# Softmax attention of 16 heads: natural units ahead of the exponentials' units, value products in up to two pieces, transposes at a chunk's end

## The chip, the core and the metric

The kernel runs on one core of one Trainium2 chip, as one launch. The time is device time in microseconds (us) of that core, and less is better. The engines named below are TensorE (PE), VectorE (DVE), ScalarE (ACT), GpSimd (POOL) and SyncE (SP), which issues DMAs.

## The reference

Four layers follow one another on x of (2, 1024, 256); the change touches the first, a differential softmax attention with 16 heads of 2 x 8 query and key columns and 16 value columns:

```python
q1, k1, q2, k2, v = jnp.split(layernorm(x) @ Wqkv, [C, 2 * C, 3 * C, 4 * C], axis=-1)
A1 = causal_sdpa(q1, k1, v)          # per head: softmax(mask(q k^T / sqrt(8))) @ v
A2 = causal_sdpa(q2, k2, v)
diff = A1 - lam * A2                 # then an RMS norm per head, and diff @ Wproj
```

After it come a routed feed-forward layer, a memory attention and a ternary feed-forward layer.

## The kernel before, in words

`attention_heads` works head by head; each engine runs its own `period(h)` for h = 0 to 15. A head has four sets: two batches b and two attentions j. The operands of j = 0 lie in partitions 0 to 63 and those of j = 1 in partitions 64 to 127 (`SIDE` = 64), so their matmuls use different row halves of TensorE.

**Natural units** (tile `nat`, three PSUM buffers) give the row maxima of the head that comes next. `unit_scores` makes one: q k^T with queries in partitions (line 644), and for a block on the diagonal two small matmuls that add the mask (line 648). DVE reduces each one (line 516, `mpart`). There are 40 to a head, alternately j = 1 (even numbers) and j = 0 (odd). When all 40 are reduced, DVE takes the head's maxima (`negm`, line 520), PE turns them (line 656), DVE splits them in three bf16 parts (lines 531 to 539), and SP moves the parts into rows of the queries, so that the exponentials' scores come out with the maximum subtracted. After that DVE goes on with the next natural units. PE starts unit u only when DVE has reduced unit u - 3.

**Units for the exponentials** (tile `sc`, two PSUM buffers) are made by `scores(h, n, c)` (line 682): keys in partitions, 9 chunks n = 0 to 8 of 512 columns, four sets c = 0 to 3 each, with j = 0, 1, 0, 1. ACT makes the exponential of each (line 611, into `PT`), and PE starts one only when the exponential of the unit two before it is done.

**Value products** (`values(h, n)`, line 702) multiply `PT` of a whole chunk with the head's values, fp32, into `OT`, all four sets side by side in column groups of 32. They come two chunks late (`VLAG` = 2): in chunk n PE does the value products of chunk n - 2, and in chunks 0 and 1 those of chunks 7 and 8 of the head before. POOL masks the diagonal chunks 0, 2, 4, 7 and 8 first (line 481). Most chunks are one segment of 512 columns; chunk 2 is 384 + 128, chunk 4 is 256 + 256, chunk 8 is 384 + 128.

When the last value products of a head are done, ACT copies `OT` out (`OTS`, line 593, after the exponentials of chunk 1), PE turns it in two halves of four **transposes** (`turn_outputs`, line 718, tile `misc`), and ACT copies each half (`ONS`, line 600) after the exponentials of chunks 2 and 3. The first value products of the new head write `OT` again, so they too wait for `OTS`.

The order on PE is written out by hand in `period`: in each of the 36 steps (n, c) a unit for the exponentials, then one natural unit (two in four of the steps: n, c = 2, 0; 4, 1; 6, 2; 8, 3), and after c = 1 the transposes (in chunks 2 and 3) and the value products. In the generator `maxima`, the turn of `negm` comes ahead of the third natural unit after a head's last, in chunk 6.

Of the kernel before, what the change touches and what calls it, by code (L numbers as in the profile page):

```python
# [351 lines left out]
def attention_heads(nc, K):  # L352
# [5 lines left out]
    NU, NCH = len(units), len(PROB_CHUNKS)  # L358
    FIRST, GAP = (2 * NU) // 5, 2
    VLAG = 2  # L360
    with ExitStack() as ctx:
# [26 lines left out]
        class Head:  # L388
# [8 lines left out]
            def next(self, d):  # L397
                return Head(self.i, self.k + d)
# [8 lines left out]
        def heads(eng, period):  # L407
            for n in range(H0):
                period(Head(0, n))

        @block.sync
        def _(sp):
            def maxima(h):

                hold(sp, s_msp, h.count(1, 1), K.s_held)
                for j in range(2):
                    for part in range(3):
                        row = SIDE * j + STK + part
                        sp.dma_start(QS[row:row + 1, h.buf, :].rearrange("a (r q) -> a r q", q=P),
                                     msplit[16 * j:16 * j + 16, part, :]).then_inc(s_mld, 16)  # L420

            def period(h):
                if h.next(2).exists():
                    if not isinstance(h.n, int) or h.n > 0:

                        hold(sp, s_sc, h.count(4 * NCH), K.s_held)
                    later = h.next(2)
                    load_head(sp, K, later.n, later.buf, slice(0, B * T), s_load[later.buf])
                if h.next(1).exists():
                    maxima(h.next(1))  # L430

            load_head(sp, K, 0, 0, slice(T, B * T), s_load[0])
            load_head(sp, K, 1, 1, slice(0, B * T), s_load[1])
            maxima(Head(0, 0))
            heads(sp, period)
# [190 lines left out]
        @block.tensor  # L626
        def _(pe):
            def unit_scores(h, u):

                head_0 = isinstance(h.n, int) and h.n == 0  # L630
                if u == 0 and head_0:
                    pe.wait_ge(K.s_first, 16 * HEAD_LOADS)
                if u == (NU // 2 if head_0 else 0):
                    pe.wait_ge(s_load[h.buf], 16 * HEAD_LOADS * (h.times + 1))

                if not isinstance(h.n, int) or NU * h.n + u > 2:
                    pe.wait_ge(s_max, h.count(NU, u - 2))
                b, j, segs = units[u]
                side, rows = slice(SIDE * j, SIDE * j + SIDE), slice(SIDE * j, SIDE * j + STK)
                for n, (i, k0, w) in enumerate(segs):  # L640
                    out = nat[:, (NU * h.k + u) % 3, n * w:(n + 1) * w]
                    q = b * T + i * P
                    diag = i * P - k0
                    ins = pe.matmul(out, QS[rows, h.buf, q:q + P], KS[rows, h.buf, b * T + k0:b * T + k0 + w],  # L644
                                    start=True, stop=diag >= w)
                    if diag < w:
                        for half, (unit, mask) in enumerate(((K.ident_bf, K.mask), (K.ident_swap, K.mask_swap))):
                            ins = pe.matmul(out[:, diag:diag + P], unit[side, :], mask[side, :], start=False, stop=half == 1)  # L648
                ins.then_inc(s_nat, 1)

            def turn_max(h):
                pe.wait_ge(s_negm, h.count(1, 1))

                if not isinstance(h.n, int) or h.n >= 2:
                    pe.wait_ge(s_ons, h.count(2, -2))
                pe.transpose(misc[0:32, 0:P], negm[:].rearrange("p j b i -> p (j b i)"), K.ident[:]).then_inc(s_mT, 1)

            def maxima(h):

                first, second = h.next(1), h.next(2)  # L660
                if not first.exists():
                    return
                for u in range(FIRST, NU):
                    unit_scores(first, u)
                    yield
                for u in range(FIRST):
                    if u == GAP or not second.exists():
                        turn_max(first)
                        if not second.exists():
                            return  # L670
                    unit_scores(second, u)
                    yield

            def scores(h, n, c):
                u = 4 * n + c
                j, b = SET_ORDER[c] // 2, SET_ORDER[c] % 2
                rows = slice(SIDE * j, SIDE * j + STK + 3)
                if not isinstance(h.n, int) or 4 * NCH * h.n + u > 1:
                    pe.wait_ge(s_exp, h.count(4 * NCH, u - 1))
                col = 0  # L680
                for kt, q0, w in PROB_CHUNKS[n]:
                    ins = pe.matmul(sc[:, u % 2, col:col + w], KS[rows, h.buf, b * T + kt * P:b * T + (kt + 1) * P],  # L682
                                    QS[rows, h.buf, b * T + q0:b * T + q0 + w], start=True, stop=True)
                    col += w
                ins.then_inc(s_sc, 1)

            def values(h, n):

                if n in DIAG_CHUNKS:
                    pe.wait_ge(s_msk, h.count(len(DIAG_CHUNKS), DIAG_CHUNKS.index(n) + 1))  # L690
                else:
                    pe.wait_ge(s_exp, h.count(4 * NCH, 4 * n + 4))
                if n == 0:
                    pe.wait_ge(s_vh, h.count(1, 1))

                    if not isinstance(h.n, int) or h.n > 0:
                        pe.wait_ge(s_ots, h.count(1))
                col = 0
                for kt, q0, w in PROB_CHUNKS[n]:
                    for c in range(4):  # L700
                        b = c % 2
                        ins = pe.matmul(OT[32 * c:32 * c + 32, q0:q0 + w], VH[:, h.buf, b * TB + kt, :],  # L702
                                        PT[:, n % 3, c, col:col + w], start=(kt == 0), stop=(kt, q0) in ((2, 256), (7, 896)),
                                        skip_group_check=True)
                    col += w
                ins.then_inc(s_pv, 1)

            def turn_outputs(h, r):
                if r == 0:
                    pe.wait_ge(s_ots, h.count(1, 1))  # L710

                    if h.next(1).exists():
                        pe.wait_ge(s_msp, h.count(1, 2))
                else:
                    pe.wait_ge(s_ons, h.count(2, 1))
                for k in range(4):
                    t = 4 * r + k
                    ins = pe.transpose(misc[:, k * P:(k + 1) * P], OTS[:, t * P:(t + 1) * P], K.ident[:])
                ins.then_inc(s_on, 1)

            def period(h):

                last, between = h.next(-1), maxima(h)

                pe.wait_ge(s_mld, h.count(96, 96))
                for n in range(NCH):
                    for c in range(4):
                        scores(h, n, c)
                        k = 4 * n + c
                        for _ in range(NU * (k + 1) // (4 * NCH) - NU * k // (4 * NCH)):  # L730
                            next(between, None)
                        if c == 1:
                            if last.exists() and VLAG <= n < VLAG + 2:
                                turn_outputs(last, n - VLAG)
                            if n >= VLAG:
                                values(h, n - VLAG)
                            elif last.exists():
                                values(last, NCH + n - VLAG)
                for _ in between:
                    pass  # L740

            for u in range(FIRST):
                unit_scores(Head(0, 0), u)
            for _ in maxima(Head(0, -1)):
                pass
            heads(pe, period)
            last = Head(0, H0 - 1)
            for n in range(VLAG):
                values(last, NCH + n - VLAG)
            for r in range(2):  # L750
                turn_outputs(last, r)
# [1704 lines left out]
```

## Time and profile before

| what | us |
|---|---|
| median of 3 runs | 1730.11 (1729.01 to 1734.66) |
| the profiled execution, its own time | 1742.41 |
| its span, first to last instruction | 1740.6 |
| stretch of the 16 heads, from the first to the last matmul of the loop | about 87 to 620 |
| one head in the middle, from one copy of `OTS` to the next | 30.98 to 31.00 |

Mean granted TensorE clock over the span: 0.926 of full speed. The profiled execution is 12.3 us above the median; differences that are worked out in its rows are subtracted from the median. The first columns of a timeline row are the start (us from the span's start) and the duration; merged rows have a count. Matmuls overlap, so the time that one takes from its neighbours is the distance from start to start, not its duration.

### The profile page before, as it was taken

The page shows a single profiled execution, that of the slowest core. Times are in us where ns is not written, and L with a number is a line of the kernel's source. Part 1 is how long each engine was busy: PE and PEld are TensorE (multiplying, and loading weights), DVE is VectorE, ACT ScalarE, POOL GpSimd, SP SyncE. Part 2 cuts the span into 40 slices and gives each one's busy share as a digit, 9 for nine tenths or more (in the row PEclk, how much of TensorE's full clock was granted, in tenths as well). Part 3 has the DMA queues.
Part 4 walks back from the last instruction along what each step waited for, and adds up shares of the span by engine and source line. Part 5 has one row for each costly group of instructions (what it writes and reads, how often), then busy time and mean ns, then how long its engine had stood idle before and what let it go on. Part 6 is the DMA issues. An engine that isn't in the chain of part 4 may idle for free. (4 is left out here: it accounts for less than half of the span.)

```text
span 1740.6 us, 27816 instructions
## 1 busy us (share of the span) xinstructions
PE 1491.9 (86%) x9044; PEld 1018.5 (59%) x9044; DVE 1261.2 (72%) x3421; ACT 1109.9 (64%) x2384; POOL 1086.0 (62%) x1283
## 2 busy tenths in 40 slices
PE   7898888888888855788856899999999999887998
PEld 4433333333333134575645788888788888776565
DVE  5778888888787025743365999999999999973433
ACT  3147767666676523403124899999999999994332
POOL 5105665655655554032243999999999999974353
PEclk9769999999999566999988999999999999999899
DMA  5301010010010041452100000000000100000000
GB/s 200 104 20 38 21 32 26 21 38 20 25 34 2 1 154 49 149 181 97 49 0 1 2 1 1 1 1 1 1 1 1 49 1 1 1 1 1 1 25 25
DMA packets 40137, 59.98 MB, mean 34 GB/s; under 512 B 9452, under 2 KB 33912, under 8 KB 39096
## 3 DMA queue, kind: packets, MB, share of 16 engines
q1 hardware_dynamic: 39992, 58.19, 10.4%
q8 instruction: 73, 1.20, 0.3%
q14 instruction: 72, 0.59, 0.1%
HBM read 40.93 MB, written 16.78 MB: 33 GB/s over the span
## 5 line engine op out<-in xcount | busy, mean ns | idle before, releaser
L611 ACT ACTIVATE a_PT<-a_sc 128x512 f32<-128x512 f32 x576 | 319.0, 599 | 209.7 <-PE a_sc L682 203.5
L516 DVE TENSOR_REDUCE a_mpart<-a_nat 128x1 f32<-128x512 f32 (+3 forms) x640 | 363.8, 628 | 87.5 <-PE a_nat L648 54.4
L2022 DVE BATCH_NORM_STATS2 c_stat<-c_R 128x6 f32<-128x512 f32 x576 | 381.1, 679 | 2.1 <-ACT c_R L1941 1.8
L1986 POOL TENSOR_SCALAR c_R<-big,c_negtau 128x256 f32<-128x256 f32 x264 | 301.4, 1168 | 34.6 <-DVE c_negtau L2055 29.0
L1986 POOL TENSOR_SCALAR c_R<-c_Z,c_negtau 128x256 f32<-128x256 f32 x255 | 291.5, 1169 | 14.9 <-DVE c_negtau L2088 14.9
L644 PE MATMUL a_nat<-mem 48*128 48x512 bf16 (+3 forms) x768 | 223.6, 356 | 25.2 <-DVE a_mpart L516 11.9
L682 PE MATMUL a_sc<-mem 51*128 51x512 bf16 (+3 forms) x768 | 207.0, 355 | 41.3 <-ACT a_PT L611 38.7
L481 POOL TENSOR_SCALAR_AFFINE_SELECT a_PT<-a_PT 128x512 f32<-128x512 f32 x128 | 79.4, 638 | 244.3 <-ACT a_PT L611 244.2
L1858 PE MATMUL c_z<-mem,c_R 128*128 128x256 f32 x1024 | 231.5, 379 | 0.0
L1941 ACT ACTIVATE c_R<-c_Z,c_negtau 128x256 f32<-128x256 f32 x513 | 216.0, 516 | 0.4 <-DVE c_negtau L2088 0.4
L1941 ACT ACTIVATE c_R<-big,c_negtau 128x256 f32<-128x256 f32 x504 | 212.6, 515 | 2.9 <-DVE c_negtau L2055 1.7
L1858 PEld LDWEIGHTS c_z<-mem,c_R 128*128 128x128 f32 x1024 | 192.9, 190 | 25.4
L702 PE MATMUL a_OT<-a_PT,a_VH 128*32 128x512 f32 (+3 forms) x1536 | 170.8, 543 | 0.6 <-POOL a_PT L481 0.6
L682 PEld LDWEIGHTS a_sc<-mem 51*128 51x128 bf16 x768 | 52.4, 95 | 197.6 <-ACT a_PT L611 158.1
L1870 PE MATMUL c_T<-ident,c_R 128*128 128x128 f32 x768 | 107.3, 283 | 36.0 <-ACT c_R L1936 35.4
L1858 PE MATMUL c_z<-mem,c_hT 128*128 128x256 f32 x512 | 119.9, 389 | 8.8 <-ACT c_hT L1965 8.8
L1882 PE MATMUL c_y<-mem,c_R 128*128 128x256 f32 x512 | 120.7, 386 | 0.0
L1870 PEld LDWEIGHTS c_T<-ident,c_R 128*128 128x128 f32 x768 | 86.5, 143 | 56.6 <-ACT c_R L1936 46.7
L1936 ACT ACTIVATE c_R<-c_T 128x512 f32<-128x512 f32 x192 | 104.2, 596 | 22.7 <-PE c_T L1870 22.7
L1858 PEld LDWEIGHTS c_z<-mem,c_hT 128*128 128x128 f32 x512 | 99.0, 195 | 24.5 <-ACT c_hT L1965 9.3
L644 PEld LDWEIGHTS a_nat<-mem 48*128 48x128 bf16 x768 | 68.1, 97 | 71.0 <-DVE a_mpart L516 50.4
L648 PE MATMUL a_nat<-mask,ident_bf 64*128 64x128 bf16 x512 | 106.9, 231 | 0.0
(316 smaller groups left out, 2638.6 us busy)
## 6 DMA issues: line engine op xcount, KB each, us to landing
mem<-qk_parts SPq DMA_DIRECT2D x360, 32.0 KB
qk_parts<-a_parts SPq DMA_DIRECT2D x16, 384.0 KB, 2.6
made<-f_made SPq DMA_DIRECT2D x24, 256.0 KB, 2.8
mem<-made SPq DMA_DIRECT2D x3, 2048.0 KB, 8.4
X<-in_L_attn_x_dram SPq DMA_DIRECT2D x4, 512.0 KB, 6.9
mem<-in_L_ffn_wq_dram SPq DMA_DIRECT2D x1, 2048.0 KB, 14.4
ternary<-f_W_T SPq DMA_DIRECT2D x1, 2048.0 KB, 6.3
mem<-in_L_ffn_wo_dram SPq DMA_DIRECT2D x1, 2048.0 KB, 12.6
```

The source lines that it names most:

```text
L516: dve.tensor_reduce(dst, src, AX.X, ALU.max).then_inc(s_max, 1)
L611: act.activation(PT[:, n % 3, SET_ORDER[c], :], sc[:, u % 2, :], ACT.Exp, scale=SCALE0).then_inc(s_exp, 1)
L644: ins = pe.matmul(out, QS[rows, h.buf, q:q + P], KS[rows, h.buf, b * T + k0:b * T + k0 + w], start=True, stop=diag >= w)
L648: ins = pe.matmul(out[:, diag:diag + P], unit[side, :], mask[side, :], start=False, stop=half == 1)
L682: ins = pe.matmul(sc[:, u % 2, col:col + w], KS[rows, h.buf, b * T + kt * P:b * T + (kt + 1) * P], QS[rows, h.buf, b * T + q0:b * T + q0 + ...
L702: ins = pe.matmul(OT[32 * c:32 * c + 32, q0:q0 + w], VH[:, h.buf, b * TB + kt, :], PT[:, n % 3, c, col:col + w], start=(kt == 0), stop=(kt ...
L1858: ins = pe.matmul(z_ps[:, n % SCORE_BANKS, e * NMEM:(e + 1) * NMEM], L, G[:, m, h, :], start=(m == 0), stop=(m == 1))
L1870: ins = pe.transpose(T_ps[:, n % TURN_BANKS, (2 * e + m) * P:(2 * e + m + 1) * P], whole(i, h)[:, m * P:(m + 1) * P], K.ident[:])
L1882: ins = pe.matmul(y_ps[:, k % 2, 0:D], weights(i, h, m), K.VO[:, m, h, :], start=(n == 0), stop=(n == 15))
L1941: act.activation(split(i, h) if r < NR else whole(i, h), scores_of(i)[:, h, :], ACT.Relu, bias=threshold(i, r, h)).then_inc(s_ra[r], 1)
L1986: pool.tensor_scalar(split(i, h) if r < NR else whole(i, h), scores_of(i)[:, h, :], threshold(i, r, h), 0.0, ALU.add, ALU.max).then_inc(s_ ...
L2022: dve.bn_stats(stat[:, r, b, :], R[:, slot(i), b, :]).then_inc(s_stat, 1)
```

## The change

In each step the natural unit now stands ahead of the unit for the exponentials. The value products are a generator that stops between segments: the first piece is issued after c = 1, the second, where there is one, after c = 2. Only chunks 2, 4 and 8 have a second piece; with the delay of two chunks these fall in chunks 4, 6 and 1. The transposes move from ahead of the value products to the end of the chunk.

```diff
             def values(h, n):
+                for _ in value_pieces(h, n):
+                    pass
+
+            def value_pieces(h, n):
...
                     col += w
+                    if col < 512:
+                        yield
                 ins.then_inc(s_pv, 1)
...
                 for n in range(NCH):
+                    pieces = value_pieces(h, n - VLAG) if n >= VLAG else value_pieces(last, NCH + n - VLAG) if last.exists() else iter(())
                     for c in range(4):
-                        scores(h, n, c)
                         k = 4 * n + c
                         for _ in range(NU * (k + 1) // (4 * NCH) - NU * k // (4 * NCH)):
                             next(between, None)
-                        if c == 1:
-                            if last.exists() and VLAG <= n < VLAG + 2:
-                                turn_outputs(last, n - VLAG)
-                            if n >= VLAG:
-                                values(h, n - VLAG)
-                            elif last.exists():
-                                values(last, NCH + n - VLAG)
+                        scores(h, n, c)
+                        if c in (1, 2):
+                            next(pieces, None)
+                    if last.exists() and VLAG <= n < VLAG + 2:
+                        turn_outputs(last, n - VLAG)
```

No instruction is added or removed. Two places of PE's order show it.

PE in chunk 2, from c = 1 to the next chunk's c = 0. Before (`nat` is a natural unit, `sc` one for the exponentials in two segments, `misc` the transposes, `OT` the value products):

```order
L682 MATMUL a1_sc<-mem3 128x384 [waits a1_exp]
L682 MATMUL a1_sc<-mem3 128x128
L644 MATMUL a1_nat<-mem3 128x512 [waits a1_max]
L718 MATMUL a1_misc<-ident,a1_OTS 128x128 [waits a1_msp,a1_ots]
L718 MATMUL a1_misc<-ident,a1_OTS 128x128 x3
L702 MATMUL a1_OT<-a1_PT,a1_VH 32x512 [waits a1_ots,a1_vh,a1_msk]
L702 MATMUL a1_OT<-a1_PT,a1_VH 32x512 x3
L682 MATMUL a1_sc<-mem3 128x384 [waits a1_exp]
L682 MATMUL a1_sc<-mem3 128x128
L644 MATMUL a1_nat<-mem3 128x512 [waits a1_max]
```

The same place in the changed kernel, up to the transposes:

```order
L682 MATMUL a1_sc<-mem3 128x384 [waits a1_exp]
L682 MATMUL a1_sc<-mem3 128x128
L706 MATMUL a1_OT<-a1_PT,a1_VH 32x512 [waits a1_ots,a1_vh,a1_msk]
L706 MATMUL a1_OT<-a1_PT,a1_VH 32x512 x3
L644 MATMUL a1_nat<-mem3 128x512 [waits a1_max]
L682 MATMUL a1_sc<-mem3 128x384 [waits a1_exp]
L682 MATMUL a1_sc<-mem3 128x128
L644 MATMUL a1_nat<-mem3 128x512 [waits a1_max]
L682 MATMUL a1_sc<-mem3 128x384 [waits a1_exp]
L682 MATMUL a1_sc<-mem3 128x128
L724 MATMUL a1_misc<-ident,a1_OTS 128x128 [waits a1_msp,a1_ots]
L724 MATMUL a1_misc<-ident,a1_OTS 128x128 x3
```

The value products now take the first wait for `OTS`, and the four transposes stand two natural units and two units for the exponentials later, ahead of the next chunk.

PE in chunk 6, from the value products on. Before:

```order
L702 MATMUL a1_OT<-a1_PT,a1_VH 32x256 x7
L682 MATMUL a1_sc<-mem3 128x512 [waits a1_exp]
L644 MATMUL a1_nat<-mem3 128x512 [waits a1_max] x2
L682 MATMUL a1_sc<-mem3 128x512 [waits a1_exp]
L644 MATMUL a1_nat<-mem3 128x512 [waits a1_max]
```

And in the changed kernel:

```order
L706 MATMUL a1_OT<-a1_PT,a1_VH 32x256 [waits a1_msk]
L706 MATMUL a1_OT<-a1_PT,a1_VH 32x256 x3
L644 MATMUL a1_nat<-mem3 128x512 [waits a1_max] x2
L682 MATMUL a1_sc<-mem3 128x512 [waits a1_exp]
L706 MATMUL a1_OT<-a1_PT,a1_VH 32x256 x4
L644 MATMUL a1_nat<-mem3 128x512 [waits a1_max]
L682 MATMUL a1_sc<-mem3 128x512 [waits a1_exp]
```

Both natural units of the double step now stand ahead of the unit for the exponentials, and the second half of the value products behind it.

## Rows read from the trace of the kernel before

**Rows 1.** Busy time in a stretch: PE, PEld, DVE, ACT, POOL, granted clock, DMA.

```profile
300.00:400.00 100.00, 88.22 (x857) 38.50 (x855) 80.60 (x161) 68.38 (x127) 58.74 (x95) 0.97 0.10 26
```

**Rows 2.** Waits of PE from 120 to 600 us: total, times, longest.

```profile
PE a_sc L682 <- ACT a_PT L611: 36.4, 91, 0.8
PE a_misc L718 <- ACT a_OTS L593: 4.3, 15, 0.3
```

**Rows 3.** Timeline of PE in one head: chunk 1 to chunk 4, and into chunk 5.

```profile
320.37 1.07 PE L702 MATMUL a_OT<-a_PT,a_VH 128*32 128x384 f32 x16
...
323.85 0.66 PE L718 MATMUL a_misc<-ident,a_OTS 128*128 128x128 f32 x4 [0.29 <-ACT a_OTS L593]
324.43 1.06 PE L702 MATMUL a_OT<-a_PT,a_VH 128*32 128x512 f32 x8
325.43 0.40 PE L682 MATMUL a_sc<-mem 51*128 51x384 bf16 x4
...
326.51 0.39 PE L682 MATMUL a_sc<-mem 51*128 51x512 bf16 x1 [0.46 <-ACT a_PT L611]
...
327.00 0.39 PE L682 MATMUL a_sc<-mem 51*128 51x512 bf16 x1
...
328.23 1.06 PE L702 MATMUL a_OT<-a_PT,a_VH 128*32 128x512 f32 x8
...
331.57 1.07 PE L702 MATMUL a_OT<-a_PT,a_VH 128*32 128x384 f32 x16
...
334.59 1.07 PE L702 MATMUL a_OT<-a_PT,a_VH 128*32 128x512 f32 x8
```

**Rows 4.** Timeline of ACT in the same head.

```profile
321.79 1.08 ACT L611 ACTIVATE a_PT<-a_sc 128x512 f32<-128x512 f32 x2 [0.78 <-PE a_sc L682]
322.76 1.03 ACT L593 ACTIVATE a_OTS<-a_OT 128x1024 f32<-128x1024 f32 x1
...
325.86 1.08 ACT L611 ACTIVATE a_PT<-a_sc 128x512 f32<-128x512 f32 x2 [1.08 <-PE a_sc L682]
```

**Rows 5.** Timeline of PE behind the value products of chunk 4.

```profile
332.58 0.28 PE L682 MATMUL a_sc<-mem 51*128 51x256 bf16 x1
332.58 0.28 PE L644 MATMUL a_nat<-mem 48*128 48x256 bf16 x1
332.70 0.27 PE L682 MATMUL a_sc<-mem 51*128 51x256 bf16 x1
```

**Rows 6.** Timeline of PE one head earlier: chunk 6 to chunk 0.

```profile
306.74 1.07 PE L702 MATMUL a_OT<-a_PT,a_VH 128*32 128x256 f32 x16
...
308.77 0.39 PE L644 MATMUL a_nat<-mem 48*128 48x512 bf16 x1 [0.64 <-ACT a_PT L611]
...
310.88 1.06 PE L702 MATMUL a_OT<-a_PT,a_VH 128*32 128x512 f32 x8
...
314.04 1.07 PE L702 MATMUL a_OT<-a_PT,a_VH 128*32 128x512 f32 x8
...
317.37 1.07 PE L702 MATMUL a_OT<-a_PT,a_VH 128*32 128x512 f32 x8
```

**Rows 7.** Timeline of DVE in that stretch.

```profile
308.04 4.26 DVE L516 TENSOR_REDUCE a_mpart<-a_nat 128x1 f32<-128x512 f32 x7
```

**Rows 8.** Timeline of ACT in that stretch.

```profile
308.17 0.60 ACT L611 ACTIVATE a_PT<-a_sc 128x512 f32<-128x512 f32 x1 [0.72 <-PE a_sc L682]
...
309.73 0.41 ACT L614 ACTIVATE a_Wabs<-Wb 128x256 f32<-128x256 bf16 x1
```

**Rows 9.** Timeline of ACT, the copies of `OTS` in the two heads that follow.

```profile
356.61 1.03 ACT L593 ACTIVATE a_OTS<-a_OT 128x1024 f32<-128x1024 f32 x1
387.60 1.03 ACT L593 ACTIVATE a_OTS<-a_OT 128x1024 f32<-128x1024 f32 x1
```

**Rows 10.** PE in a stretch: busy time, granted clock, DMA.

```profile
345.00:349.00 4.00, 4.00 (x22) 0.50 0.02 4
```

**Rows 11.** Timeline of PE in that stretch, the value products of chunk 6.

```profile
346.55 1.93 PE L702 MATMUL a_OT<-a_PT,a_VH 128*32 128x512 f32 x8
348.41 0.80 PE L682 MATMUL a_sc<-mem 51*128 51x384 bf16 x3
```

## The prediction

> **What bounds the kernel now.** I read first the busy times of a stretch of the heads: TensorE 88 of 100 us, DVE 81, ACT 68, POOL 59, at a granted clock of 0.97 [rows 1]. No engine is full, so each waits for others in turn. The list of TensorE's waits then says for whom: 36.4 us in 91 waits for exponentials, and 4.3 us in 15 waits for the copy of the outputs [rows 2]. The timelines of one head show where these fall.
>
> I count a head by its value products; V(n) are those of chunk n. One head: V(8) at 320.37, V(0) at 324.43, V(1) at 328.23, V(2) at 331.57, V(3) at 334.59 [rows 3]; a head earlier V(4) at 306.74, V(5) at 310.88, V(6) at 314.04, V(7) at 317.37 [rows 6]. The distances are 4.06, 3.80, 3.34, 3.02, then 4.14, 3.16 and 3.33.
>
> The distance of a plain chunk is a loop through ACT, not TensorE's work. From V(0): the value products hold the array from 324.43 to 325.43, 1.00 us. The next unit for the exponentials starts at 325.43; its exponential starts at 325.86, 0.43 later [rows 4]. Two exponentials take 1.08, so the second starts 0.48 after the first and lasts 0.60. It ends at 326.94, and the unit for c = 1 of the next chunk starts at 327.00, 0.06 later [rows 3]. With one natural unit more the next V could follow, at 1.00 + 0.43 + 1.08 + 0.06 = 2.57 plus 0.3 to 0.6. Before c = 0 TensorE stood idle, a wait of 0.46 by the row at 326.51. So the transposes, 0.58 us ahead of V(0) and as much ahead of V(1) (323.85 to 324.43 [rows 3]), stand on the loop where nothing covers them, while 0.46 us of idle time lie half a chunk later.
>
> Chunks 5 to 7 are different: DVE does seven natural units without a gap from 308.04, 0.61 each [rows 7], after it has split the maxima. TensorE waits for it.
>
> **The change part by part.** No instruction comes or goes, DMAs are untouched, and POOL and SP keep their places. I follow the new order with the durations above. Two more are needed. Value products take 1.00 at full clock and 346.55 to 348.41 = 1.86 at the granted clock of 0.50 [rows 10, 11]. So 0.86 scales with the columns and 0.14 does not: a piece of 384 columns takes 0.64 + 0.14 = 0.78, one of 128 takes 0.36, one of 256 takes 0.57. A natural unit or one for the exponentials holds its row half for 0.22 (estimate from the four that fill 325.43 to 326.3), one with masks 0.33. I allow 0.1 for entering value products or transposes.
>
> *A, V(8) to V(0), 4.06 before.* The transposes leave: -0.58. V(0) now has the wait for `OTS` itself. V(8) comes in pieces of 384 and 128. The first lets the unit c = 2 start 0.22 earlier, but the second piece and its entry, 0.46, stand ahead of c = 3. Its exponential starts 0.78 + 0.22 + 0.46 + 0.43 = 1.89 after V(8), against 321.79 + 0.48 - 320.37 = 1.90 now. `OTS` is no earlier [rows 3, 4]. A = -0.58.
>
> *B, V(0) to V(1), 3.80 before.* The natural unit that now comes first is odd (j = 0), on the same row half as the unit c = 2, so that one starts at 1.22. Exponentials at 1.65 and 2.13, end 2.73; unit c = 1 at 2.79, V(1) at 2.79 + 0.32 = 3.11. The transposes (0.56 and 0.2 for entry and exit) are issued at 1.55, finish near 2.3 and delay c = 0 (ready at 2.31) hardly. B = -0.69.
>
> *C, V(1) to V(2), 3.34 before.* The same loop with masks, start of c = 2 at 1.33, gives 3.2, and now the second transposes stand in it: TensorE is nearly full. C = -0.14.
>
> *D, V(2) to V(3), 3.02 before.* The second piece delays c = 3, and V(3) comes at 3.28. But DVE takes the outputs' small operations and four short units there, and in my follow-through its next long unit starts at 4.8 after V(2), as before. D = +0.04, bounds -0.1 and +0.27.
>
> *E, chunk 6.* The trace has natural unit 5, second of the double step, waiting until 308.77 for DVE (the row's releaser names ACT; it starts 0.05 after DVE's unit 2 ends, 308.04 + 0.68) [rows 6, 7]. Behind it on TensorE stands c = 3 now. After the change c = 2 does too: its exponential, at 308.17 before [rows 8], comes at 308.77 + 0.22 + 0.43 = 309.4. Then comes the second piece of V(4), to 309.88, the unit c = 3 at 310.1, its exponential 310.5 to 311.1, with ACT's operation for the ternary weights (0.41 [rows 8]) behind it. So c = 1 of chunk 7 starts at 311.17 and V(5) at 311.5, against 310.88. DVE takes up part of it, since its backlog ends near 312.3 in either order: V(6) comes at 314.6 against 314.04. E = +0.55, bounds 0 and +0.8.
>
> *F, V(6) to V(8).* In chunks 8 to 1 c = 1 has no natural unit between it and the value products, which saves the 0.11 of the masks once or twice; a natural unit ahead of c = 2 can cost as much. F = -0.1, bounds -0.3 and +0.3.
>
> Sum for a head: -0.58 - 0.69 - 0.14 + 0.04 + 0.55 - 0.1 = -0.92. It holds 14 times (heads 1 to 14 for A to C, 0 to 13 for E), -12.9 us. In the last head, with no natural units, the clock is low, the transposes are twice as long against the same idle time, and the pieces delay c = 3 longer: I take 0. Its own time 1742.4 would become 1729.5, the median 1730.1 becomes **1717**. POOL's mask of chunk 0 and SP's loads have microseconds to spare and see a period 3% shorter.
>
> If the whole cover failed (no idle time for the transposes, so A to C = 0), the head would gain nothing and lose D and E: +0.5.
>
> **Two rules weighed.** Whether a unit for the exponentials can start beside a natural unit that stands ahead of it decides part of F and D. The trace has a natural matmul starting at 332.58, while the second matmul of the unit ahead of it starts at 332.70 [rows 5]. So the two row halves run past each other, at least over a matmul or two, and the sum uses that. The Trainium skill (TensorE: Matmul & The Clock Gate, Part 3: Packing small matmuls) says otherwise: matmuls start and end strictly in program order. By that rule alone the score would start only after the last mask, and the result would be that of the second rival. The Trainium skill (TensorEngine Tiling (Array Packing), Tiling Modes) also says that changing the tiling mode drains TensorE. The change adds five such visits for pieces and transposes to a head. The trace agrees with a cost, the 0.14 above.
>
> **The rivals.**
>
> 1. *E does not bite.* DVE's backlog hides chunk 6 altogether, and F comes out at its good end. For it: DVE is the slow one there. Against: ACT then stands still over 1 us, and its loop sets V(6). -1.5 a head, -21 us: **1709**. Chance 0.18.
>
> 2. *Units wait behind masks.* If c = 2 starts only after the masks ahead of it (0.28, or 0.38 for two blocks), three or four chunks per head are longer by about 0.15 to 0.2 net: +0.6 a head, so -0.3, -4 us: **1726**. For it: these units come first in chunks 0, 4 and 5. Against: [rows 5]. Chance 0.12.
>
> 3. *Only a rotation.* TensorE's sequence is nearly the old one turned by half a step, and the transposes lose elsewhere what they gain: **1730**. Against: the idle 0.46 at 326.51. Chance 0.07.
>
> 4. *Slower: the clock falls in more heads.* Behind chunks 6 and 7, where TensorE does little, the granted clock fell to 0.50 [rows 10], and that head took 356.61 - 322.76 = 33.85 against 30.99 for the next [rows 4, 9]. That is 2.9 us; three of the 14 heads do so. E makes the thin stretch thinner. Gain and loss balance at 12.9 / 2.9 = 4 to 5 more such heads. If all 14 did it, 11 more at about 2.5 less the 12.9 gives +15: **1745**. Against: chunks 0 to 4 become denser. Chance 0.09.
>
> **How the numbers follow.** The forecast itself, 1711 to 1724, has 0.54. A measurement of this kernel tells about 0.3%, 5.2 us. Faster: the forecast, rival 1 and part of rival 2, 0.76; within 0.3%: most of rivals 2 and 3, 0.16; slower 0.08. The range leaves out the far ends of rivals 1 and 4: 1706 to 1727. A to F at their bounds alone give -1.8 to 0 a head, which is 1705 to 1730.
>
> **What would show it.** Copies of `OTS` 30.0 to 30.1 apart. V(8) to V(0) 3.5, V(0) to V(1) 3.1, V(1) to V(2) 3.2. The wait of TensorE for exponentials well under 36.4, and that for `OTS` at the value products. In chunk 6 an exponential at least 1 us later than before, and V(4) to V(6) longer by about half a microsecond. The prediction is wrong if chunks 2 and 3 keep their lengths, if V(4) to V(6) stays at 7.30, or if more than four heads have value products of 1.93 us.

## The result, and the profile after

| | before | changed |
|---|---|---|
| median, us | 1732.38 (1729.01 to 1738.37) | 1758.91 (1754.43 to 1760.11) |
| the profiled execution's own time | 1742.41 | 1754.43 |
| its span | 1740.6 | 1752.7 |
| mean granted clock of the span | 0.926 | 0.909 |

The ratio is 1.0145, with a 95% interval of 1.0108 to 1.0181. The change made the kernel slower by about 1.5%, where a median of 1717 us, 0.8% faster, was forecast.

The busy times of the stretch that stands in [rows 1] are now, for the changed kernel (PE, PEld, DVE, ACT, POOL, granted clock, DMA):

```profile
300.00:400.00 100.00, 93.27 (x806) 36.58 (x809) 79.48 (x157) 66.95 (x124) 57.69 (x94) 0.90 0.09 28
```

TensorE is busy 93 instead of 88 us, with fewer instructions, at a clock of 0.90 instead of 0.97: it is not fuller of work, its work takes longer. TensorE's waits from 120 to 600 us, which answer to [rows 2]:

```profile
PE a_nat L644 <- DVE a_mpart L516: 15.6, 20, 1.1
PE a_sc L682 <- ACT a_PT L611: 8.7, 24, 0.8
PE a_OT L706 <- ACT a_OTS L593: 5.1, 15, 0.4
```

The wait for exponentials has gone from 36.4 to 8.7 us, as the change would have it, and the one for `OTS` now stands at the value products. The waits of natural units are fewer and longer. In the kernel before they were, in the same view:

```profile
PE a_nat L644 <- DVE a_mpart L516: 9.9, 44, 0.9
PE a_nat L644 <- ACT a_PT L611: 7.6, 12, 0.6
```

That is 17.5 us in 56 waits, against 15.6 in 20, and the longest has gone from 0.9 to 1.1 us. The timeline of TensorE from one head into the next where nothing disturbs it, for [rows 3]:

```profile
167.09 0.85 PE L706 MATMUL a_OT<-a_PT,a_VH 128*32 128x384 f32 x8
...
168.19 0.43 PE L706 MATMUL a_OT<-a_PT,a_VH 128*32 128x128 f32 x8
...
170.67 1.07 PE L706 MATMUL a_OT<-a_PT,a_VH 128*32 128x512 f32 x8 [0.34 <-ACT a_OTS L593]
...
172.21 0.66 PE L724 MATMUL a_misc<-ident,a_OTS 128*128 128x128 f32 x4
...
173.77 1.06 PE L706 MATMUL a_OT<-a_PT,a_VH 128*32 128x512 f32 x8
...
176.98 0.85 PE L706 MATMUL a_OT<-a_PT,a_VH 128*32 128x384 f32 x8
...
180.34 1.06 PE L706 MATMUL a_OT<-a_PT,a_VH 128*32 128x512 f32 x8
```

V(8), V(0), V(1), V(2), V(3) are 3.58, 3.10, 3.21 and 3.36 apart, where they were 4.06, 3.80, 3.34 and 3.02. The copies of `OTS` around that boundary, at 139.40 and 169.50, are 30.10 apart. So the new order saves nearly what the sum said while the clock is up. That holds for the first three heads; from the fourth on a head without a fall of the clock takes 30.30, since the wait of chunk 6, described below, is 1.07 us there and 0.87 in the first three. What the change costs is seen in the timeline of ACT further on, the copies of `OTS` around one later head:

```profile
231.22 1.02 ACT L593 ACTIVATE a_OTS<-a_OT 128x1024 f32<-128x1024 f32 x1
...
266.42 1.02 ACT L593 ACTIVATE a_OTS<-a_OT 128x1024 f32<-128x1024 f32 x1
```

That head took 35.20. The timeline of TensorE in it, V(4) to V(5):

```profile
245.07 0.64 PE L706 MATMUL a_OT<-a_PT,a_VH 128*32 128x256 f32 x8
...
247.11 0.39 PE L644 MATMUL a_nat<-mem 48*128 48x512 bf16 x1 [1.07 <-DVE a_mpart L516]
...
247.64 0.64 PE L706 MATMUL a_OT<-a_PT,a_VH 128*32 128x256 f32 x8
...
250.04 1.94 PE L706 MATMUL a_OT<-a_PT,a_VH 128*32 128x512 f32 x8
```

And TensorE's busy time, granted clock and DMA in stretches of 4 us of the same head:

```profile
245.00:249.00 4.00, 2.93 (x25) 1.00 0.02 3
249.00:253.00 4.00, 3.89 (x17) 0.51 0.02 3
253.00:257.00 4.00, 3.95 (x23) 0.50 0.01 2
257.00:261.00 4.00, 4.00 (x35) 0.50 0.13 35
261.00:265.00 4.00, 4.00 (x36) 0.79 0.27 82
```

The reader is to see the order of events. Between the two pieces of V(4) TensorE waits 1.07 us for DVE. From 249.0, 1.4 us after the second piece starts, the clock is at 0.5, that is 1.2 GHz instead of 2.4, and stays there for 13.7 us, although TensorE is busy nearly all of that time. V(5) takes 1.94 instead of 1.06.

The order of events does not yet show what the fall depends on. Two heads of the changed kernel, the eighth and the last of the 13, have the same wait of 1.07 and no fall; the first row below is the 4 us from V(4) on in the eighth, and the second the same 4 us of the head shown above:

```profile
382.05:386.05 4.00, 2.92 (x25) 1.00 0.02 3
245.07:249.07 4.00, 2.93 (x25) 1.00 0.02 3
```

In the kernel before the same stretch (306.74 to 310.74) is busy for less, 2.74 us. Neither the wait nor the busy share around it decides for a single head; the experiments can only say how often and how long the clock falls.

The account from the first to the 14th copy of `OTS` (13 heads): before, 410.3 us, 13 x 30.98 and 7.5 of falls in three heads; changed, 426.4 us, 3 x 30.10 + 10 x 30.30 = 393.3 and 33.1 of falls in nine heads, eight of which lose 3.6 to 4.9 us. The order gave 9.4 us and the falls took 25.6. Worked out from the granted clock in steps of 1 us, the clock was low for 6.8 us in each fall of before; in the changed kernel it was low for 3.4 us in one, 10.2 us in six and 13.7 us in two. The last two heads took 69.2 us before (granted clock 0.75 and 0.51) and 60.6 after (0.90 and 0.65). The parts ahead of the first copy and behind the last are 2.6 and 2.0 us longer; with them the 12 us between the profiled executions are accounted for. The profiled execution of before is 10.0 us above its median and that of the changed kernel 4.5 below, so the medians are 26.5 apart; the balance lies in runs without a trace.

### The profile page after: what moved, and what is told of

It is laid out like the page before. It is cut to its first block and busy times, and to the rows that moved or that the text cites. A ratio compares the mean times of both kernels' runs of the same rounds, so it can differ in the third digit from the quotient of the medians.

```text
span 1752.7 us, 27817 instructions
## 1 busy us (share of the span) xinstructions
PE 1530.1 (87%) x9044; PEld 1019.9 (58%) x9044; DVE 1263.0 (72%) x3421; ACT 1111.5 (63%) x2384; POOL 1084.3 (62%) x1283
## 5 line engine op out<-in xcount | busy, mean ns | idle before, releaser
L644 PE MATMUL a_nat<-mem 48*128 48x512 bf16 (+3 forms) x768 | 236.7, 374 | 25.0 <-DVE a_mpart L516 17.6
L682 PE MATMUL a_sc<-mem 51*128 51x512 bf16 (+3 forms) x768 | 214.6, 367 | 14.1 <-ACT a_PT L611 11.7
L706 PE MATMUL a_OT<-a_PT,a_VH 128*32 128x512 f32 (+3 forms) x1536 | 189.6, 569 | 6.8 <-ACT a_OTS L593 5.1
L1874 PE MATMUL c_T<-ident,c_R 128*128 128x128 f32 x768 | 106.7, 282 | 36.4 <-ACT c_R L1940 35.8
L648 PE MATMUL a_nat<-mask,ident_bf 64*128 64x128 bf16 x512 | 111.8, 238 | 0.0
L648 PE MATMUL a_nat<-mem 64*128 64x128 bf16 x512 | 110.6, 235 | 0.0
```

The lines of the kernel that those rows point to most:

```text
L1874: ins = pe.transpose(T_ps[:, n % TURN_BANKS, (2 * e + m) * P:(2 * e + m + 1) * P], whole(i, h)[:, m * P:(m + 1) * P], K.ident[:])
```

## The experiments

A fall is a head longer than its kernel's undisturbed one. The table is read from one trace of each kernel. Its second column is the length of an undisturbed head; where two lengths stand, the first is that of the first three heads. The third is TensorE's longest wait in chunk 6, for DVE's natural units, in the same way. The fourth is the sum of the excess in the 13 heads from the first to the 14th copy of `OTS`, with the number of heads that have a fall; the fifth is the length of the last two heads together. Before is 1732 to 1735 in each comparison.

| kernel | head at full clock | wait in chunk 6 | lost, 13 heads (falls) | last two heads | median, us |
|---|---|---|---|---|---|
| before | 30.98 | 0.62 to 0.65 | 7.5 (3) | 69.2 | 1732.4 |
| changed | 30.10, 30.30 | 0.87, 1.07 | 33.1 (9) | 60.6 | 1758.9 |
| transposes alone (e1) | 29.89 | 0.60 to 0.63 | 11.3 (6) | 57.7 | 1718.7 |
| natural units alone (e2) | 30.99 | 0.61 to 0.65 | 7.4 (3) | 67.5 | 1733.7 |
| pieces alone (e3) | 31.30 | 0.81 | 17.6 (7) | 68.3 | 1752.2 |
| natural units and transposes (e4) | 29.54, 29.75 | 0.44, 0.65 | 12.5 (8) | 57.8 | 1720.2 |
| changed, with filler (e5) | 30.29 | none over 0.2 | 0.0 | 59.1 | 1716.4 |
| before, with filler (e6) | 30.98 | 0.21 | 0.3 (0) | 63.9 | 1727.7 |
| transposes, with filler (e7) | 29.91 | 0.21 | 0.3 (0) | 62.8 | 1710.0 |
| changed, V(4) whole (e9) | 29.72, 29.92 | 0.44, 0.64 | 13.6 (7) | 58.1 | 1722.6 |
| V(4) in pieces alone (e10) | 31.36 | 1.03 to 1.06 | 25.5 (10) | 64.4 | 1761.9 |
| changed, second piece early (e11) | 29.72, 29.92 | 0.30, 0.51 | 17.2 (7) | 59.0 | 1727.2 |
| e4 with filler (e12) | 29.82 | 0.21 | 0.0 | 60.9 | 1710.9 |
| e12 with filler at the end too (e14) | 29.82 | 0.21 | 0.0 | 55.2 | 1705.0 |

In the kernel before, e1, e6, e7 and e10 the seventh head is out of line: chunk 6 comes about 0.35 us later there, and without filler its wait is 0.2 longer than the table says (0.87 before), because DVE is late. The 0.3 of e6 and e7 is this head, at a granted clock of 1.00; it is no fall.

My theory after the result was the clock: the order saves time, and a longer wait in chunk 6 lets the clock fall in more heads. The rivals: that any shorter head brings the falls, and that one of the three parts alone does. The first four runs take the change apart and test the clock itself.

**Transposes alone.** The kernel before with

```diff
-                            if last.exists() and VLAG <= n < VLAG + 2:
-                                turn_outputs(last, n - VLAG)
...
+                    if last.exists() and VLAG <= n < VLAG + 2:
+                        turn_outputs(last, n - VLAG)
```

> The kernel before with one part of the change: the transposes at the end of the chunk. Theory 1 (the order saves time at full clock, and the loss comes from chunk 6, where natural units ahead of the exponentials' units and the second piece of the value products make TensorE's thin stretch thinner, so that the granted clock falls in more heads): chunk 6 is as before, so falls stay at 0 to 4 heads; the head at full clock takes 29.6 us against 30.99, time 1732 - 20 = 1712, range 1706 to 1722. Theory 2 (any shorter head brings the falls, whatever chunk 6 holds): 29.6 us at full clock too, but 8 to 10 heads with a fall of 4 us each, time 1735 to 1755.

Measured 1718.74, ratio 0.9929 (0.9911 to 0.9947). V(8) to V(0) became 3.58 and V(0) to V(1) 3.21; the rest stayed. All of the gain at full clock, 1.1 us a head, is this part's. Six heads have a fall, more than before, but of 1.1 to 2.6 us each: a shorter head with nearly the same wait did have a few more falls, cheap ones. The head itself is 0.3 longer than I expected of either theory.

**Natural units alone.**

```diff
-                        scores(h, n, c)
                         k = 4 * n + c
...
+                        scores(h, n, c)
```

> The kernel before with one part of the change: each natural unit ahead of the unit for the exponentials. Theory 1: the head at full clock takes 31.0 to 31.3, the exponential of chunk 6, c = 2 comes late as in the changed kernel, and the clock falls in 6 to 10 heads: time 1750 to 1775. Theory 2: the head is no shorter, so falls stay at 3 or so: 1730 to 1738.

Measured 1733.69, ratio 1.0008 (0.9993 to 1.0023): no difference, at the same 30.99 a head. V(4) to V(5) is longer by 0.2 (4.34), other chunks shorter by as much. The longest wait of chunk 6 stays at 0.61 to 0.65, and there are three falls, not 6 to 10. My first theory, as far as it blamed this part, is wrong.

**Pieces alone.** The changed kernel with the other two parts undone.

```diff
+                    if col < 512:
+                        yield
...
+                        if c == 1 and last.exists() and VLAG <= n < VLAG + 2:
+                            turn_outputs(last, n - VLAG)
+                        if c in (1, 2):
+                            next(pieces, None)
```

> The kernel before with one part of the change: the value products in two pieces where the chunk has two segments. The head at full clock takes 31.0 to 31.6. Theory 1: the second piece of V(4) stands behind TensorE's wait for VectorE in chunk 6, so its wait starts 0.4 us earlier; falls in 3 to 8 heads, time 1735 to 1760. Theory 3 (the pieces are without effect, the falls come from the natural units alone): 1728 to 1740, falls in 3 heads.

Measured 1752.21, ratio 1.0120 (1.0101 to 1.0139). A head at full clock is 0.3 us longer, and seven of 13 have a fall, of 1.2 to 3.7 us, within what was expected if the second piece of V(4) lengthens the wait.

**The changed kernel with a filler.** Two matmuls whose result no one reads, where TensorE waits.

```diff
+                            if n == 6 and c == 2 and i == 1 and h.next(2).exists():
+                                for _ in range(2):
+                                    pe.matmul(misc[64:128, 256:512], K.ident[:, 64:128], K.X[:, 0, :], start=True, stop=True)
                             next(between, None)
```

> The changed kernel with two matmuls more per head that no one reads (fp32, 256 columns, into a free part of the transposes' PSUM tile), between the two natural units of chunk 6, c = 2, where TensorE waits about 0.9 us for VectorE. If the loss is the clock that falls behind that wait (theory 1), they hold it up: falls in 0 to 4 heads, a head still 30.1 us, time 1715 to 1735. If the falls have another cause, they stay at 8 to 9 heads and the time is 1752 to 1765.

Measured 1716.44, ratio 0.9910 (0.9886 to 0.9934): 42 us under the changed kernel, for work added. The timeline of TensorE in its chunk 6:

```profile
148.48 0.64 PE L706 MATMUL a_OT<-a_PT,a_VH 128*32 128x256 f32 x8
149.05 0.39 PE L644 MATMUL a_nat<-mem 48*128 48x512 bf16 x1
149.36 1.08 PE L739 MATMUL a_misc<-X,ident 128*64 128x256 f32 x4
150.50 0.39 PE L644 MATMUL a_nat<-mem 48*128 48x512 bf16 x1
```

and its copies of `OTS` in the timeline of ACT, for the head with the 35.20 above:

```profile
225.53 1.02 ACT L593 ACTIVATE a_OTS<-a_OT 128x1024 f32<-128x1024 f32 x1
...
255.83 1.02 ACT L593 ACTIVATE a_OTS<-a_OT 128x1024 f32<-128x1024 f32 x1
```

The filler takes the place of the wait, and the head takes 30.30. All 13 heads take 30.28 to 30.31, at a granted clock of 1.00. That is 0.2 more than an undisturbed head of the changed kernel in the first three, and no more in the others, and all falls are gone. This shows that the loss is the clock, and that the falls hang on what TensorE does around the wait in chunk 6.

**Which piece, and why.** Two runs ask whether V(4)'s second piece is the one, and whether the splitting or the place matters. First, V(4) whole again:

```diff
-                    if col < 512:
+                    if col < 512 and n != 4:
```

> The changed kernel with the value products of chunk 4 whole again; the pieces of chunks 2 and 8 stay. If the falls of the granted clock come from the second piece of V(4) alone: a head at full clock 29.9 us, falls in 2 to 4 heads as in the kernel before, time 1712 to 1722. If the other two pieces or the shorter head bring them as well: 1735 to 1755.

Measured 1722.63, ratio 0.9940 (0.9916 to 0.9963). The time is 0.6 us above the upper end of what I gave for "V(4) alone", and the count is not that of it: seven of 13 heads have a fall, six of 1.3 to 1.6 us and one of 5.1. So V(4)'s piece mostly makes the falls long: without it seven heads fall instead of nine, and lose 13.6 us instead of 33.1.

Second, still two pieces, but the second one ahead of the natural unit that waits:

```diff
+                            if n == 6 and i == 1:
+                                next(pieces, None)
                             next(between, None)
```

> The changed kernel with the second piece of V(4) moved ahead of the natural unit that waits for VectorE in chunk 6; it is still two pieces. If the length of that one wait (0.87 us in the changed kernel, 0.64 before) decides on the clock: the wait shrinks to 0.3 to 0.5, falls in 0 to 4 heads, time 1708 to 1724. If it is the splitting itself that thins TensorE's work: falls stay at 7 to 9 heads, 1745 to 1760.

Measured 1727.15, ratio 0.9948 (0.9925 to 0.9971). The timeline of TensorE in its chunk 6:

```profile
149.64 0.64 PE L706 MATMUL a_OT<-a_PT,a_VH 128*32 128x256 f32 x8
150.21 0.39 PE L644 MATMUL a_nat<-mem 48*128 48x512 bf16 x1
150.52 0.64 PE L706 MATMUL a_OT<-a_PT,a_VH 128*32 128x256 f32 x8
151.47 0.39 PE L644 MATMUL a_nat<-mem 48*128 48x512 bf16 x1 [0.30 <-DVE a_mpart L516]
```

The wait is 0.30 in the first three heads, as here, and 0.51 in the others, instead of 0.87 and 1.07. Five of the seven falls are back to 1.2 to 1.5 us, but two of 5.1 remain, both in heads with a wait of 0.51. The time is 3 us above what I gave for "the wait decides" and 32 us under the changed kernel. So splitting does little harm, and splitting around the wait does. But a short wait does not abolish falls, and this kernel loses no less than e9 with its longer wait: the length of the wait alone does not set the loss.

**Natural units and transposes, without pieces.** Both diffs of the first two runs together.

> The change without the pieces: natural units first and transposes at the end of the chunk. All theories that blame the pieces: a head at full clock 29.7 us (V(4) to V(5) 4.33 as with the natural units alone), falls in 3 to 5 heads, time 1712 to 1720, equal to the transposes alone (1718.7) or up to 4 us better. If a shorter head with a late exponential in chunk 6 brings falls of its own: 1730 to 1750.

Measured 1720.15, ratio 0.9911 (0.9884 to 0.9938), the same as the transposes alone. The time is what the theories that blame the pieces gave, but the count of falls is not: eight heads instead of 3 to 5, all but one of 1.3 to 1.6 us.

**Transposes with the filler.**

> The kernel before with the transposes at the end of the chunk and the two matmuls that no one reads in chunk 6. The transposes alone gave 29.88 us a head and five heads with falls that cost 1.2 to 2.6 us each. If the filler holds the clock up whatever the order around it: no falls, 29.9 a head, time 1706 to 1712. If it only mended what the pieces had done: 1716 to 1721 as without it.

Measured 1710.02, ratio 0.9849 (0.9821 to 0.9876). No falls in 13 heads; the filler works without the pieces and with the natural units in their old place too.

**The kernel before with the filler.**

> The kernel before with the two matmuls that no one reads in chunk 6. Control for the filler: if it holds the clock up whatever the order, all heads take 30.98 to 31.05, the three falls of 2.2 to 2.9 us go, time 1720 to 1730; beside the changed kernel with the filler (30.29 a head, 1716) this gives the worth of the new order at full clock, which the prediction put at 0.92 us a head: 0.6 to 0.8 here, 9 to 12 us. If the filler costs TensorE time of its own here, 31.2 and 1733 to 1738.

Measured 1727.73, ratio 0.9964 (0.9945 to 0.9984). The heads take 30.96 to 31.00, but for one of 31.32. The filler costs nothing here, since it fits into the wait, and the three falls are gone as expected. With the filler in both, the new order is worth 30.98 - 30.29 = 0.69 us a head and 1727.7 - 1716.4 = 11.3 us in the medians, as expected; by the ratios to the kernel before, which allow for the two being measured in different comparisons, 0.9964 and 0.9910, it is about 9 us.

**V(4) in pieces, nothing else.**

```diff
-                    if col < 512:
+                    if col < 512 and n == 4:
```

on the kernel with the pieces alone.

> The kernel before with V(4) alone in two pieces, in the old order, so that the second piece stands behind the natural unit that waits for VectorE. If that one piece is the cause: a head at full clock 31.1, falls in 5 to 8 heads, time 1742 to 1755, near the 1752 of all pieces. If the pieces of V(2) and V(8) matter: 1731 to 1738.

Measured 1761.91, ratio 1.0160 (1.0122 to 1.0197), the slowest of all. The timeline of TensorE in its chunk 6:

```profile
220.81 0.64 PE L706 MATMUL a_OT<-a_PT,a_VH 128*32 128x256 f32 x8
221.38 0.39 PE L682 MATMUL a_sc<-mem 51*128 51x512 bf16 x1
221.39 0.39 PE L644 MATMUL a_nat<-mem 48*128 48x512 bf16 x1
222.83 0.60 PE L644 MATMUL a_nat<-mem 48*128 48x512 bf16 x1 [1.06 <-DVE a_mpart L516]
223.36 1.08 PE L706 MATMUL a_OT<-a_PT,a_VH 128*32 128x256 f32 x8
```

The wait is 1.06, and behind it everything already takes nearly twice as long: 0.60 for a natural matmul instead of 0.39, 1.08 for the second half of V(4) instead of 0.64. Ten of 13 heads have a fall, of 1.3 to 3.7 us; the other three have the same wait without one. That one piece is enough to lose as much as the whole change did: of the 30 us, 0.38 a head, 5 in all, are longer heads at full clock, and the profile shows 18 us more of falls in 13 heads. The time and the count came out above what I had expected (1742 to 1755, 5 to 8 heads), and above all pieces together (1752, seven heads, with a wait of 0.81 instead of 1.05).

**Best versions.** Natural units, transposes and filler:

> Natural units first, transposes at the end, no pieces, and the filler. Without it 29.55 to 29.76 us a head with eight falls of 1.3 to 2.4 us, 1720. If the filler holds the clock: 29.75 to 29.95 a head, time 1704 to 1711, equal to or up to 4 us under the 1710 of the transposes with filler. If natural units first makes the filler too small to hold it: 1715 to 1720.

Measured 1710.85, ratio 0.9870 (0.9843 to 0.9898): every head 29.82. The last two heads still lose time to the clock, so the last run adds one matmul of the same kind, behind a wait for the copies of `misc`, to eight of their 18 chunks:

```diff
+                    if not h.next(2).exists() and (n > 6 or h.n == H0 - 1 and n not in (2, 3, 4)):
+                        pe.wait_ge(s_ons, h.count(2) if n > 4 else h.count(2, -2))
+                        pe.matmul(misc[64:128, 256:512], K.ident[:, 64:128], K.X[:, 0, :], start=True, stop=True)
```

> As the kernel before it, with one more matmul that no one reads in most chunks of the last two heads, where there are no natural units and the clock was at half in the kernel before (34.35 and 34.86 us a head). If it keeps the clock up there: 27.5 to 28.5 for each of them, time 1698 to 1706. If it only lengthens them, because the clock is up without it in most runs: the same time or up to 3 us more.

Measured 1705.02, ratio 0.9836 (0.9807 to 0.9864): the fastest, 54 us under the changed kernel and 27 under the one before. The last two heads take 28.9 and 26.3 (27.5 to 28.5 each was expected), at a granted clock of 1.00 and 0.90, against 31.3 and 29.7 at 0.85 and 0.64 without.

## Why the prediction was wrong

*The sum at full clock was nearly right.* Forecast -0.92 us a head, measured 30.10 - 30.98 = -0.88 in the first three heads and 30.30 - 30.98 = -0.68 in the others. The lengths of the pieces were right: 0.78, 0.36 and 0.57 from start to the next matmul, as the sum had them. By terms, in the first head: A -0.48 (forecast -0.58), B -0.70 (-0.69), C -0.13 (-0.14). D, taken on to V(4), is 3.36 + 3.02 against 3.02 + 3.14, +0.22 (+0.04): DVE's work does not hide all of V(2)'s second piece. E, V(4) to V(6), is 153.25 to 160.90 = 7.65 against 7.30, +0.35 (+0.55); the first exponential behind V(4) starts 2.47 after it instead of 1.43. In the eighth head, with the wait of 1.07, E is +0.54 and that exponential comes 2.67 after V(4), as followed through (2.66). F, V(6) to V(8), is 6.19 against 6.33, -0.14 (-0.1).

*The step that failed is that the sum had no term for more falls of the clock: they stood only in the fourth rival, with too small a chance and too low a price.* I wrote that "E makes the thin stretch thinner" and gave more falls 0.09; more and longer falls are what happened, nine heads instead of three, and 25.6 us of loss against a gain of 9.4. The price was too low as well: I took 2.5 to 2.9 us for a fall from heads in which the clock was low for 6.8 us, and eight heads, with 10.2 or 13.7 us at the low clock, lost 3.6 to 4.9. Even that rival's far end, 1745, is 14 us short. With nine falls the sum could only end slower: six more at 2.5 us are 15 us. And "thinner" was not right as a busy share: TensorE is busy 2.93 us of the 4 from V(4) on, against 2.74 before. What grew is the one wait. I had also sized E by when V(6) comes, not by how long TensorE stands still between the halves of V(4): with half of V(4) ahead of the waiting unit, TensorE reaches that wait 0.43 us sooner while DVE ends it at nearly the same time. The wait grows from 0.64 to 0.87 or 1.07. The rows allowed that to be read: 1.00 for the whole, 0.57 for the half, and the end of the wait at 308.77 set by DVE.

*The part I thought risky was harmless.* The natural units first cost nothing (e2), neither by E nor by waiting behind masks (rival 2). By the Trainium skill's rule of program order (TensorE: Matmul & The Clock Gate, Part 3) I had put the cost at 0.6 a head. With natural units alone a head stayed at 30.99, so nothing of that cost shows.

*The medians.* The profiled execution of before was 10.0 us above its median and that of the changed kernel 4.5 below, so the profiles show the change as less bad than the medians do. The last two heads of before (69.2 us, against 60.6) may hold the 10 us; no trace of a run at the median shows it.

*Open.* Why a shorter head has six to eight falls, most of them small, where the old one has three, with a wait in chunk 6 that is no longer (e1, e4, e9), why two long ones remain with a wait of 0.51 (e11), and why of heads with the same wait some fall and some do not, no run tells apart. So it is shown that the second piece of V(4) behind the wait brings the loss and that the filler removes falls of both kinds; that the length of the wait is what the clock answers to is argued, not shown.

## What to carry to other kernels

Where TensorE waits for another engine once per round, ask what an edit does to that one wait, not only to the critical path: putting half of the work ahead of it behind it, which made it 0.4 us longer once in 31 us, cost 30 us of 1732, most of it through the clock (e10). Work placed into the wait, even matmuls that no one reads, can be worth more than a reordering: here 42 us on the changed kernel, where the best reordering without it gave 15 (e1, e4). Try it as an experiment before an order is judged. And price a fall of the clock with room above the worst head of the trace: here that head lost 2.9 us, and the changed kernel's lost up to 4.9.

## What the runs showed of the hardware

The granted clock fell to 0.5 behind single waits of 0.87 to 1.07 us between value products, with TensorE busy 2.9 to 3.1 of 4 us around them, in nine of 13 heads of the changed kernel; in four heads with the same waits it stayed at 1.00. It fell behind shorter waits too, down to 0.30 us, in three to eight heads of 13 (before, e1, e2, e4, e9, e11). It stayed low for 6.8 us in each of the three falls of the kernel before and for 10.2 or 13.7 us in eight heads of the changed one; in the one of 13.7 us that was followed, TensorE was busy 3.9 to 4.0 of every 4 us by then. Two fp32 matmuls of 256 columns per head, 1.08 us at the place of the wait, kept it at 1.00 for all of 13 heads (394 us). In the last two heads, eight such matmuls in all raised it from 0.85 and 0.64 to 1.00 and 0.90.
